# Projection products ahead of the short score products in every third attention step of a decoder layer

## The reference

```python
qkv = x @ w_qkv                         # 32 query heads, 8 key heads, 8 value heads, 32 features each
xq, xk = _apply_rope(xq), _apply_rope(xk)
keys, values = jnp.repeat(xk, 4, axis=1), jnp.repeat(xv, 4, axis=1)
scores = jnp.einsum('bhsd,bhtd->bhst', xq, keys) * scale
scores = jnp.where(causal, scores, -jnp.inf)
out = jnp.einsum('bhst,bhtd->bhsd', jax.nn.softmax(scores, axis=-1), values)
x = _layernorm(x + out.reshape(8, 256, 1024) @ w_o)
```

## Time and profile before

| | |
|---|---|
| median of 3 timed runs | 1259.14 us (1256.8 to 1260.54) |
| the profiled execution | 1260.72 us |
| its span, first to last instruction | 1257.9 us |
| mean granted clock of TensorE | 0.993 of full speed |
| busy share of the span | PE 98%, weight loads 83%, DVE 69%, POOL 49%, ACT 46% |

### The profile page before, as it was taken

One profiled execution on the slowest core, in us unless ns is written; L12 is line 12 of the kernel. 1 busy time (PEld: TensorE's weight loads), 2 busy tenths in 40 slices (PEclk: granted clock), 3 DMA queues, 4 the chain that ended last, 5 costly groups with the idle time before them and its releaser, 6 DMA issues.

```text
span 1257.9 us, 23612 instructions
## 1 busy us (share of the span) xinstructions
PE 1232.7 (98%) x8134; PEld 1041.5 (83%) x8134; DVE 862.9 (69%) x2510; ACT 580.6 (46%) x1659; POOL 615.5 (49%) x520
## 2 busy tenths in 40 slices
PE   8999999999999999999999999999999999899997
PEld 6888889998778888888877787888888888788886
DVE  7999989565877888788776973344363625866564
ACT  5131213556777777877760121342342524632322
POOL 3512112458666776776750000454556454975552
PEclk9999999998999999999999999999999999999999
DMA  8154436363864444435433112427243354633221
GB/s 287 70 201 146 148 117 204 118 202 125 223 186 140 119 137 139 130 119 149 129 120 128 38 50 101 151 68 252 79 156 116 132 204 151 217 134 117 86 83 67
DMA packets 130870, 174.12 MB, mean 138 GB/s; under 512 B 36672, under 2 KB 91968, under 8 KB 130112
## 3 DMA queue, kind: packets, MB, share of 16 engines
q1 hardware_dynamic: 130752, 172.62, 42.0%
HBM read 115.94 MB, written 56.62 MB: 137 GB/s over the span
## 4 chain that ended last, share of the span: by engine, by line
PE 88%; DVE 6%; POOL 2%; ACT 1%; DMA 1%; issue 1%; SPq 1%; POOLq 0%; DVEq 0%; ACTq 0%
PE bank L966 14%; PE bank L775 12%; PE bank L777 12%; PE bank L776 12%; PE bank L903 6%; PE bank L888 5%; PE bank L861 5%; PE bank L1206 4%; PE bank L1208 4%; PE bank L1207 4%; PE bank L931 3%; PE bank L826 2%; PE bank L784 1%; PE bank L935 1%; DVE bits L1674 1%
## 5 line engine op out<-in xcount | busy, mean ns | idle before, releaser
L2176 POOL TENSOR_TENSOR prob<-prob,rinv 128x512 f32<-128x512 f32 x192 | 206.8, 1078 | 149.1 <-DVE rinv L1761 149.0
L1328 ACT ACTIVATE prob<-bank,nmax 128x256 f32<-128x256 f32 (+1 forms) x512 | 211.6, 430 | 77.8 <-DVE nmax L1753 76.9
L1753 DVE CUSTOM_DVE_ANT_0 bank<-bank,mask 128x256 f32<-128x256 f32 (+1 forms) x512 | 170.3, 385 | 36.3 <-issue 26.8
L903 PE MATMUL bank<-ident,prob 128*128 128x128 f32 x768 | 115.9, 274 | 2.3 <-POOL prob L2176 1.5
L903 PEld LDWEIGHTS bank<-ident,prob 128*128 128x128 f32 x768 | 94.9, 141 | 26.5 <-POOL prob L2176 3.3
L1328 ACT ACTIVATION_READ_ACCUMULATOR prob<-bank,nmax 128x1 f32 x512 | 109.8, 214 | 0.0
L1908 DVE SCALAR_TENSOR_TENSOR k_lo<-bank,bA,k_hi 128x512 fp32r<-128x512 f32 x32 | 24.0, 751 | 122.1 <-ACT k_hi L1461 120.7
L966 PE MATMUL bank<-wo_hi,att_hi 128*128 128x512 f32 x256 | 104.4, 408 | 2.5 <-issue 2.5
L888 PE MATMUL bank<-k,q 96*128 96x256 f32 (+1 forms) x512 | 104.3, 306 | 1.0 <-DMA vv<-v_scr 0.9
L966 PE MATMUL bank<-wo_hi,att_lo 128*128 128x512 f32 x256 | 101.6, 397 | 0.0
L966 PE MATMUL bank<-wo_lo,att_hi 128*128 128x512 f32 x256 | 101.6, 397 | 0.0
(11 more groups left out here) (221 smaller groups left out, 3252.4 us busy)
## 6 DMA issues: line engine op xcount, KB each, us to landing
q<-qk_scr SPq DMA_DIRECT2D x192, 128.0 KB, 2.5
x_st<-x_scr SPq DMA_DIRECT2D x32, 512.0 KB, 4.5
qk_scr<-rot SPq DMA_DIRECT2D x60, 256.0 KB, 2.7
xc_in<-x_cols SPq DMA_DIRECT2D x32, 256.0 KB, 4.7
y<-x SPq DMA_DIRECT2D x16, 512.0 KB, 3.6
x_scr<-y SPq DMA_DIRECT2D x16, 512.0 KB, 3.4
cx_in<-ctx_in SPq DMA_DIRECT2D x16, 512.0 KB, 4.8
x_scr<-x_st SPq DMA_DIRECT2D x16, 512.0 KB, 2.9
```

Source lines behind the costliest of these rows:

```text
L903: mm = nc.tensor.transpose(tb[:, at * P:(at + 1) * P], prob[:, k % 4, c:c + P], ident[:, :])
L1328: mm = nc.scalar.activation(prob[:, k % 4, i * keys:(i + 1) * keys], SBANK[pos][:, i * keys:(i + 1) * keys], ACT.Exp, bias=nmax[:, k % 4, ...
L1753: mm = nc.vector.tensor_tensor_reduce(part, part, mask[:, 2 * P - keys:2 * P], 1.0, BIGGEST, ALU.add, ALU.min, nmax[:, k % 4, i:i + 1])
L2176: nc.gpsimd.tensor_tensor(pr, pr, rinv[:, k % 4, 0:n].unsqueeze(2).to_broadcast([P, n, keys]), ALU.mult)\
```

## The change

In `stage2_batch` of the matrix engine, in steps with k % 3 == 2, `scores(b, k)` moves behind `fill`, `turn_last` and `project_step`, and so stands right ahead of `turn_probs`. Nothing is added or removed; the other two steps of a unit, the other engines and the waits of each instruction stay as they are. There are 64 such steps, 8 in each batch; in the 8 of batch 0 it is the `fill` products that go first.

```diff
             def stage2_batch(b, age):
 
                 for k in range(SUB):
-                    scores(b, k)
+                    if k % 3 < 2:
+                        scores(b, k)
                     if age == 0:
                         fill(k)
                     if age == 0 and k in TURN_LAST:
                         turn_last(TURN_LAST[k])
                     project_step(b, k, age)
+                    if k % 3 == 2:
+                        scores(b, k)
                     if age or k >= LAG:
                         late(b, k - LAG, turn_probs)
                     if age or k >= PV_LAG:
```

## The result

The changed kernel takes 1288.52 us (median of 5 runs, 1286.12 to 1289.49), the kernel before 1259.37 us (5 runs, 1256.8 to 1261.78): a ratio of 1.023, 95% interval 1.022 to 1.0241. It is 29 us slower. The profiled execution of after took 1286.12 us with a span of 1284.1 us, against 1260.72 and 1257.9 before: +25.4 and +26.1. The forecast was 1281.7 us, with a range of 1268 to 1294 us, and slower.

The account below looks back on a forecast made before the run. PE was taken as the bound, with late helpers stalling it. Terms 14.7 + 1.4 + 6.9 + 0.6 + 0.8 - 1.0 - 0.8 = +22.6 us on 1259.14 gave 1281.7 us, range 1268 to 1294.

Parts of the forecast that it names:

- PE's own order: Third step on PE: an even trade of exposed loads, -0.013 us a unit, about 62 units, -0.8 us.
- The gap: 0.20 us on PE before the score loads: given to the switch of weight width, so it stays.
- rival 1: The 0.20 us gap belongs to the scores and goes with them: 1271.5 us, 9%.
- Maxima 0.79 later, and 0.47 of margin at the turn: DVE's maxima delay ACT's probT copy past its spare time; second-step turn stalls 0.32 us a unit.
- It comes back each unit: PE issues the scores itself, so the turn's stall repeats: 14.7 us over 46 units, 1.4 in batch 1.
- rival 3: The stall is paid once a batch, as ACT and DVE then stay ahead: 1261 us, 10%.
- POOL's att_lo: Projection at k = 2 and k = 5 waits 0.63 and 0.64 us for POOL: 6.9 us in all.
- rival 2: DVE's late rinv delays parts of y; four units of eight pay 0.79 us, not 0.32: 1294 us, 10%.
- rival 4: Projection loads taken during the gap, -19 us, if the copy comes less than 0.47 us later: 1240 us, 5%.
- The edges: Batch 0 hidden, 0 (at most +1); batch 1, k = 2, +0.6; end of batch 7, +0.8; vv load, -1.0.
- The tail: The end of batch 7 hangs on the same ACT copy: +0.8 us.
- The DMA term: The vv load holds PE 1.11 us at 363.82; if DMA keeps its time, earlier stalls are swallowed: -1.0 us.

Follow-up runs that it names:

- the split kernels: Changed kernel with two, or three, of the four projection products ahead of the scores in third steps, the rest behind: 1269.61 us and 1278.05 us.
- the kernel with batch 0 alone: Kernel before with the new order in batch 0 only, scores behind the fill products: 1260.57 us, ratio 1.0015.
- the one with the tile moved: Changed kernel, ACT's copy and POOL's att_lo first, batch 0's old order, one w_o tile's low half moved to batch 1's step 2: 1256.64 us; repeated, 1258.34.
- two products ahead: Changed kernel with two of four projection products ahead of the scores in third steps and two behind, from batch 1 on: 1269.61 us, ratio 1.008.
- the kernel with the tile's move alone: Kernel before with only POOL's low half of one w_o tile moved from batch 0's step 22 to batch 1's step 2: 1258.86 us, ratio 1.0001.

## Why the prediction was right

**PE's own order: right.** It was put at -0.013 us a unit. From the last weighted product's start to the first score product behind the third step it was 2.029 us in the unit of the earlier trace rows and is 2.013 in its twin (2.04 and 2.01 on average where nothing waits); a batch without stalls lasts 47.97 us, not 48.07, so -0.10 for eight units. The first score load, a 96-row load behind a 512-column product that no row showed, is hidden: last projection product at 535.79, the first score product at 536.03, 0.24 later.

**The gap: right.** 0.20 us ahead of L966 after, 0.20 ahead of L888 before, 0.17 ahead of the weighted loads in both. So rival 1 falls. By the Trainium skill (TensorEngine Tiling (Array Packing), Key Properties), a change of tiling mode drains the engine. The rows agree, with 0.17 and 0.20 us at the two switches, and the 0.20 stays the same whichever full-width work comes next; that the gap is the drain, no run shows by itself.

**Maxima 0.79 later, and 0.47 of margin at the turn: right.** Counted from the unit's first load, the maxima were due at 1.72 us and start at 1.73. A little luck is in that: they start 0.41 us behind the last short score product, not 0.36, and that product comes 0.04 us sooner than walked. The turn was due at 5.01 and starts at 5.01. The stall was put at 0.32 us; units went from 6.01 to 6.36 us, so +0.35, or 0.37 beside the 5.99 of a unit of the new order without a stall. The recorded idle time is only 0.17 us, for the reason given above. The threshold that the split kernels show, about 0.57 us of delay for the scores, fits the prediction: 0.13 us of it the maxima never saw, since DVE was busy for so long, and 0.47 is the margin, 0.60 together.

**It comes back each unit: right.** All of the units in batches 3 to 6 show it, so rival 3 (paid once) falls.

**POOL's att_lo: right.** 0.63 and 0.64 predicted, 0.65 and 0.63 measured in the units' lengths, 1.29 a batch by its removal. That the `att_lo` at k = 3 stays covered was right too: no wait stands there. Without the turn's stall the two waits grew to 0.99 each.

**DVE passes its lateness on (rival 2): no.** One unit of eight in a batch has maxima 0.44 behind the scores, not 0.41, and lasts 6.37 to 6.38 us, not 6.36; that is all. The mechanism exists, as the units with scores at k = 17 in the split kernels show, but there it only spoils a margin. With four products ahead the scores are so late that DVE has nothing left to be late with.

**Faster (rival 4): no.** It needed the gap and the chain to be otherwise, and both were as the rows said.

**The middle of the stage.** Batches 3 to 6 were put at 8 x 0.32 + 2 x 0.64 less 0.1 = +3.7 us each; they cost 4.15. That is 0.05 in each of eight units and +1.6 us in all, within the 0.06 that I allowed for each. About 0.01 of it is a term that I counted twice: in a unit whose length is set by the wait (5.01 to the turn and 1.31 behind it, 6.32) the 0.013 that the order gains can't show. About 0.03 comes behind the wait: the second turn product follows the first by 0.14 us (540.01 to 540.14), where it was 0.11 (510.94 to 511.04).

**The edges: the step that failed.** "Hidden, 0 (at most +1)" for batch 0 looked inside batch 0, where it was right (92.09 us against 92.28). The cost sits in the first steps of batch 1: rinv of step 19 behind the maxima of step 20, POOL without a spare moment from there on, and the turn of step 22. That is 1.7 us by the time of the kernel with batch 0 alone (0.4 to 3.4 by its interval) and 0.97 by the length of batch 1 in its trace. The second term that failed is batch 2: I took half of its POOL waits, as POOL is earlier there, but both stand in full, with 0.61 us idle at 364.97 and 0.56 at 371.93. Together batches 1 and 2 cost +6.1 where the sum had +3.5 (1.4 + 0.6 in batch 1; seven stalls, half of the POOL waits and the -1.0 in batch 2; the order's -0.2). I had followed the moved step's own chain and not the work of another step queued behind it, although I had done exactly that for ACT's copy. The tail, predicted at +0.8, came to +1.2: batch 7's 4.87 less 3.66 in its seven full units.

**The DMA term.** The -1.0 for stalls swallowed by the `vv` load has this against it: the load's wait is in the trace of before (0.9 us, at the start of batch 2) and not at that place in after's, but it is there or absent from one trace to the next of the same kernel (batch 2 of the one with the tile moved took 47.97 us in one trace and 49.33 in the other). I can't say that the term was right.

**The sum.** +22.6 predicted, +27.4 in the stage, +26.1 in the span, +25.4 in the profiled executions and +29.2 in the medians. The missing 4.8 us in the stage are 2.6 from batches 1 and 2, 1.6 from the middle and 0.7 from batch 7, less 0.1. The medians differ by 3.8 us more than the two profiled executions: that of before lay 1.35 us above its median, and that of after was the fastest of its five, 2.40 below. The 6.9 us for POOL is 7.0 by its own count (11 x 0.64). The rest of the program is 1.3 us shorter in after's trace; one part of that is a spell of 3.4 us in which PE ran at half the clock, at 779 us, that the trace of before has and that of after hasn't.

## What to carry to other kernels

When work moves on the engine that sets the time, take the engines that prepare its next operands in their own order, and ask for each late operation what stands right behind it there, of other steps too: here PE waited for a copy of older turns, for the scaling of a step that was not moved and for the low half of an older pair, none of which reads the moved scores. Follow such an engine until it has spare time: at the border of batches 0 and 1, POOL carried the lateness of one rinv for 13 us. A margin is a threshold: cost an edit by the delay less the margin, times the number of repetitions, and expect that the next wait grows by what the first one gives back. The order that is cheapest on PE alone (0.1 us a batch here) isn't worth 0.9 us of lateness on three helpers.

## What the runs showed of the hardware

The Trainium skill (Perfetto Trace Analysis, Tensor Engine Instruction (MATMUL, LD_WEIGHTS)) states that ACT, DVE and GpSimd are strict FIFO. The runs agree, and show what that costs: moving one ACT copy ahead of four exponentials that wait gave back 16.2 us, and moving two POOL operations of 1.3 us ahead of a waiting one 9.5 us.

A weight load starts 0.11 us behind the end of the ACT copy that it waits for, whether or not PE was kept waiting (539.87 to 539.98 after; 528.89 to 529.00 with two products ahead, where PE wasn't late), and 0.05 us behind POOL's end.

The granted clock fell to its lower level (1.2 GHz) once in batch 1 of the kernel before, at 307.7 us for 6.8 us, within PE's idle time of 2.55 us that ends at 308.49. All nine traces with the tile in its old place have a spell there, of 3.4 to 10.2 us, and their longest idle time beside it is 2.04 to 3.13 us. In the four traces with the tile moved, the longest is 1.33 to 1.70 us, and the clock stays at 2.4 GHz. An idle time of about that length doesn't always bring a spell: with two products ahead PE was idle for 2.03 us at 1104.5, and the clock stayed up. What a spell costs beside the idle time was not measured by itself: the kernel with the tile's move alone has lost it, and its batch 1 is 0.67 us shorter, idle time included.
